# A cross-attention and mixture-of-experts layer on one core: normalised tiles split before they are turned, and turned by DMA

## The reference

```
x = x + xattn(layernorm(x), ctx)          # 16 heads of 32, causal, softmax over 64 keys
x = x + ffn(layernorm(x))
ffn(x):  logits = x @ router_w.T          # 8 experts, top 2 taken, weighted by their logits
         y_e = (silu(x @ wg_e) * (x @ wu_e)) @ wd_e
         out = sum of the chosen y_e * logit  +  shared expert (with biases)
```

## Time and profile before

| | us |
|---|---|
| runs shown | 870.81, 870.39, 866.59; median 870.39 |
| the profiled execution | 872.62 |
| its span in the trace | 870.9 |
| mean granted clock of TensorE | 0.979 of full |
| busy: TensorE, VectorE, ScalarE, GpSimd | 791.0, 614.5, 439.7, 429.2 |

### The profile page before, as it was taken

One profiled execution on the slowest core, in us unless ns is written; L12 is line 12 of the kernel. 1 busy time (PEld: TensorE's weight loads), 2 busy tenths in 40 slices (PEclk: granted clock), 3 DMA queues, 4 the chain that ended last, 5 costly groups with the idle time before them and its releaser, 6 DMA issues.

```text
span 870.9 us, 22280 instructions
## 1 busy us (share of the span) xinstructions
PE 791.0 (91%) x7516; PEld 545.4 (63%) x7516; DVE 614.5 (71%) x1196; ACT 439.7 (50%) x805; POOL 429.2 (49%) x530
## 2 busy tenths in 40 slices
PE   4478988989898989898999999999999999999994
PEld 1367776777777768687787787545555455455552
DVE  4978886989898989886557877555555555555552
ACT  3375766777777777777533553333333333333331
POOL 1144856565656656654600001255555555656553
PEclk9789998999999999999999999999999999999998
DMA  9324272635353534334575666488989889988892
GB/s 316 107 73 144 98 218 96 203 118 201 101 211 112 193 118 127 111 108 134 189 249 183 196 197 204 105 142 147 157 145 154 147 142 160 145 146 148 144 149 42
DMA packets 102760, 132.39 MB, mean 152 GB/s; under 512 B 54368, under 2 KB 55392, under 8 KB 101280
## 3 DMA queue, kind: packets, MB, share of 16 engines
q1 hardware_dynamic: 86784, 95.74, 37.3%
q0 software_dynamic: 15904, 35.70, 24.2%
HBM read 71.61 MB, written 52.31 MB: 142 GB/s over the span
## 4 chain that ended last, share of the span: by engine, by line
PE 46%; DVE 6%; ACT 4%; DMA 4%; issue 3%; POOL 3%; POOLq 0%; another core or an unknown queue 0%; ACTq 0%; DVEq 0%; SPq 0%
PE psum L1264 34%; PE psum L1312 8%; PE psum L1255 4%; DMA hidT<-xn2T_f 3%; DVE head_max L995 1%; DVE xy L1005 1%; DVE stats L926 1%; ACT probsT L700 1%; POOL rstd L532 1%; POOL kv_store L568 1%; ACT xn2T L700 1%; DVE w_q L1244 0%; PE psum L1364 0%; DVE hid L1219 0%; ACT attnT L700 0%
## 5 line engine op out<-in xcount | busy, mean ns | idle before, releaser
L680 POOL DMA_INDIRECT out<-w_q,tabs x71 | 112.5, 1584 | 109.1 <-DVE w_q L1244 72.9
L670 POOL DMA_INDIRECT x_in<-normed_tokens,tabs x71 | 71.0, 1000 | 137.6 <-DVE tabs L1130 88.2
L1229 DVE SCALAR_TENSOR_TENSOR hid<-psum,tabs,silu_g 128x256 f32<-128x256 f32 x71 | 34.4, 484 | 110.3 <-ACT silu_g L824 110.3
L1264 PE MATMUL psum<-exp_all,hidT 128*128 x426 | 103.4, 379 | 4.7 <-DMA hidT<-xn2T_f 4.7
L824 ACT ACTIVATE silu_g<-psum,tabs 128x256 f32<-128x256 f32 x71 | 33.7, 474 | 145.0 <-PE psum L1264 134.8
L1312 PE MATMUL psum<-xn1T,w_q 128*128 128x128 f16 x1536 | 93.3, 222 | 6.7 <-DVE xn1T L862 6.7
L1264 PE MATMUL psum<-exp_all,probsT 128*128 x420 | 96.4, 379 | 0.0
L1312 PEld LDWEIGHTS psum<-xn1T,w_q 128*128 128x128 f16 x1536 | 88.5, 99 | 7.1 <-DVE xn1T L862 6.9
L1264 PE MATMUL psum<-w_o,attnT 128*128 128x512 f16 x384 | 88.7, 381 | 0.0
L1264 PEld LDWEIGHTS psum<-exp_all,hidT 128*128 128x128 f16 x426 | 41.7, 98 | 55.8 <-issue 7.7
L530 POOL TENSOR_SCALAR rstd<-moments 128x1 f32<-128x1 f32 x64 | 14.3, 223 | 120.2 <-DVE moments L931 112.8
(11 more groups left out here) (199 smaller groups left out, 1730.2 us busy)
## 6 DMA issues: line engine op xcount, KB each, us to landing
x_in<-x SPq DMA_DIRECT2D x64, 256.0 KB, 3.1
exp_all<-experts SPq DMA_DIRECT2D x8, 1536.0 KB, 8.5
out<-xy SPq DMA_DIRECT2D x32, 256.0 KB, 2.1
normed_tokens<-xn SPq DMA_DIRECT2D x32, 256.0 KB, 2.4
normed_turned<-xn2T SPq DMA_DIRECT2D x32, 256.0 KB, 2.0
w_q<-out SPq DMA_DIRECT2D x32, 256.0 KB, 2.9
out<-w_q SPq DMA_DIRECT2D x32, 256.0 KB, 2.6
probsT<-normed_turned SPq DMA_DIRECT2D x16, 256.0 KB, 3.4
```

Source lines behind the costliest of these rows:

```text
L670: pool.indirect_dma_start(x_in[:, t % 4, :], None, xn_dram, bass.IndirectOffsetOnAxis(gather_at[:, t:t + 1], 0)).then_inc(gathered[t % 4], 16)
L680: pool.indirect_dma_start(out, bass.IndirectOffsetOnAxis(add_at[:, t:t + 1], 0), y[:, t % Y_RING, :], None, bounds_check=TOKENS - 1, oob_i ...
L1229: dve.scalar_tensor_tensor(hid[:, :], psum[:, GU_BANK[m % 2], I:2 * I], up_scale_at[:, tm:tm + 1], silu_g[:, :], ALU.mult, ALU.mult).then_ ...
L1264: last = pe.matmul(dst, lhsT(a, c), rhs(z, c), start=(c == 0 and a == z == 0), stop=(c == n - 1 and a == 1))
```

## The change

Both normalised tiles are split on ScalarE (high) and GpSimd (low) while still unturned, into `xn1p` and `xn2p`, and SP turns both halves of a tile with one transposing DMA of 128x1024 float16. TensorE's eight transposes per step, three ScalarE copies from PSUM and VectorE's low half of `xn1T` are gone. The scale by 2^11 moves into the inverse deviation. The expert's weights arrive in three DMAs, in steps j = 0, 1, 2. On ScalarE, qT and the logits now come ahead of xn2; on VectorE the magnitudes come behind qT; SP stores `xn2T` one step later. Two of the four `hidT` buffers lie in `xn1p`, and `hid_parts` in `xn2p`.

```diff
+EXPERT_PARTS = ((0, GU // 2), (GU // 2, GU // 2), (GU, WE - GU))
...
-        hidT = sb("hidT", [P, 4, 2, CI, P], F16)
-        xn2T_f = sb("xn2T_f", [P, H])
-        hid_parts = xn2T_f[:, :].bitcast(F16).rearrange("p (r v i) -> p r v i", r=2, v=2)
+        xn1p = sb("xn1p", [P, 2, H], F16)
+        hidT_store = sb("hidT_store", [P, 2, 2, CI, P], F16)
+        hidT = [hidT_store[:, n, :, :, :] for n in range(2)] + [
+            xn1p[:, n, :].rearrange("p (v c q) -> p v c q", v=2, c=CI) for n in range(2)]
+        xn2p = sb("xn2p", [P, 2, H], F16)
+        hid_parts = xn2p[:, :, :].rearrange("p r (v i) -> p r v i", v=2)
...
@@ SP, step @@
                 if live(t3):
                     load_again(t3, j + 1)
+                if live(t6):
+                    sp.wait_ge(xn2_turned, 16 * (t6 + 1))
+                    sp.dma_start(xT_dram[bass.ds(t6 * P, P), :], xn2T[:, :, :, :].rearrange("p v c q -> p (v c q)")
+                                 ).then_inc(xT_stored, 16)
+                if live(t1):
+                    sp.wait_ge(xn1_parts, t1 + 1)
+                    wait(sp, q_mm, t1)
+                    sp.dma_start_transpose(xn1T[:, :, :, :].rearrange("p v c q -> p (v c) q"),
+                                           xn1p[:, :, :].rearrange("p v h -> p (v h)")).then_inc(xn1_turned, 16)
...
-                if j == 0 and e is not None:
-                    sp.wait_ge(expert_in, 16 * e)
-                    load_expert(e)
+                if j < 3 and e is not None:
+                    sp.wait_ge(expert_in, 16 * (3 * e + j))
+                    load_expert(e, j)
...
-                    sp.wait_ge(xn2T_ready, t5 + 1)
-                    sp.dma_start(xT_dram[bass.ds(t5 * P, P), :], xn2T[:, :, :, :].rearrange("p v c q -> p (v c q)")
-                                 ).then_inc(xT_stored, 16)
+                    sp.wait_ge(xn2_parts, t5 + 1)
+                    wait(sp, router_mm, t5)
+                    wait(sp, xT_stored, 16 * t5)
+                    sp.dma_start_transpose(xn2T[:, :, :, :].rearrange("p v c q -> p (v c) q"),
+                                           xn2p[:, :, :].rearrange("p v h -> p (v h)")).then_inc(xn2_turned, 16)
...
@@ GpSimd, inv_std @@
-                pool.tensor_scalar(rstd[:, which, 0:1], moments[:, which, 1:2], EPS, None, ALU.add).then_inc(ln_eps[which], 1)
+                pool.tensor_scalar(rstd[:, which, 0:1], moments[:, which, 1:2], EPS, X_UP ** -2, ALU.add, ALU.mult
+                                   ).then_inc(ln_eps[which], 1)
...
@@ GpSimd, step: at its start, and in place of the old subtraction @@
+                if live(t1):
+                    pool.wait_ge(xn1_hi, t1 + 1)
+                    pool.tensor_tensor(xn1p[:, 1, :], xn1[:, :], xn1p[:, 0, :], ALU.subtract).then_inc(xn1_parts, 1)
                 if live(tile):
                     inv_std(0, tile)
...
-                    pool.wait_ge(xn2T_hi, 2 * (t5 + 1))
+                    pool.wait_ge(xn2_hi, t5 + 1)
...
-                    pool.tensor_tensor(flat(xn2T[:, 1, :, :]), xn2T_f[:, :], flat(xn2T[:, 0, :, :]),
-                                       ALU.subtract).then_inc(xn2T_ready, 1)
+                    pool.tensor_tensor(xn2p[:, 1, :], xn2[:, (j + 1) % 2, 0:H], xn2p[:, 0, :],
+                                       ALU.subtract).then_inc(xn2_parts, 1)
...
@@ ScalarE, step: xn2 moved behind qT and the logits; then attnT, and @@
+                if live(t5):
+                    act.wait_ge(xn2_ready, t5 + 1)
+                    wait(act, xn2_turned, 16 * t5)
+                    copy(xn2p[:, 0, :], xn2[:, (j + 1) % 2, 0:H], 1.0, xn2_hi)
...
@@ (probsT as before) @@
-                if live(t5):
-                    act.wait_ge(xn2T_mm, t5 + 1)
-                    wait(act, xT_stored, 16 * t5)
-                    copy(flat(xn2T[:, 0, :, :]), bank(6), X_UP, xn2T_hi)
-                if live(t1):
-                    act.wait_ge(xn1T_mm, t1 + 1)
-                    copy(flat(xn1T[:, 0, :, :]), bank(7), X_UP, xn1T_hi)
-                if live(t5):
-                    wait(act, xn2T_ready, t5)
-                    copy(xn2T_f[:, :], bank(6), X_UP, xn2T_hi)
...
                 if live(tile):
                     act.wait_ge(ln_rstd[0], tile + 1)
+                    wait(act, xn1_parts, tile)
                     act.activation(xn1[:, :], x_in[:, j % 2, 0:H], ACT.Identity, bias=rstd[:, 0, 2:3],
                                    scale=rstd[:, 0, 1:2]).then_inc(xn1_ready, 1)
+                    act.wait_ge(xn1_ready, tile + 1)
+                    wait(act, xn1_turned, 16 * tile)
+                    copy(xn1p[:, 0, :], xn1[:, :], 1.0, xn1_hi)
...
@@ VectorE, step: magnitudes moved behind qT, and @@
-                if live(t1):
-                    dve.wait_ge(xn1T_hi, t1 + 1)
-                    low(flat(xn1T[:, 1, :, :]), bank(7), X_UP, flat(xn1T[:, 0, :, :]), xn1T_ready)
...
@@ VectorE, entry @@
-                    low(flat(xgT[n % 4][:, 1, :, :]), bank(XG_BANK[t % 2]), X_UP, flat(xgT[n % 4][:, 0, :, :]), xgT_ready)
+                    dve.tensor_tensor(flat(xgT[n % 4][:, 1, :, :]), bank(XG_BANK[t % 2]), flat(xgT[n % 4][:, 0, :, :]),
+                                      ALU.subtract).then_inc(xgT_ready, 1)
...
@@ TensorE, step @@
-                    pe.wait_ge(xn1T_ready, t2 + 1)
+                    pe.wait_ge(xn1_turned, 16 * (t2 + 1))
...
-                    pe.wait_ge(xn2T_ready, t6 + 1)
+                    pe.wait_ge(xn2_turned, 16 * (t6 + 1))
+                    wait(pe, logits_ready, t6)
...
-                if live(t5):
-                    pe.wait_ge(xn2_ready, t5 + 1)
-                    wait(pe, logits_ready, t5)
-                    transposes(bank(6), xn2[:, (j + 1) % 2, :], C, xn2T_mm)
-                if live(t1):
-                    pe.wait_ge(xn1_ready, t1 + 1)
-                    wait(pe, xn1T_ready, t1)
-                    transposes(bank(7), xn1[:, :], C, xn1T_mm)
```

More of the change, by code:

```diff
@@ L367, in load_again, with load_expert @@
                 sp.dma_start(x_in[:, 2 + j % 2, 0:H], x[bass.ds(tile * P, P), :]).then_inc(xr_loaded[j % 2], 16)
[L369 to L371 removed]
+            def load_expert(e, n):
+                start, size = EXPERT_PARTS[n]
+                sp.dma_start(exp_raw[:, bass.ds(e * WE + start, size)],
+                             experts[:, bass.ds(e, 1), start:start + size].rearrange("p o w -> p (o w)")
+                             ).then_inc(expert_in, 16)
             def through_dram(e):
@@ L457, in _ @@
             sp.dma_start(sd_bias[:, :], sd_b.partition_broadcast(P)).then_inc(bias_in, 16)
-            load_expert(0)
+            for n in range(3):
+                load_expert(0, n)
             for b in range(3):
@@ L582, in step @@
                 tile = TPB * b + j
-                t2, t3, t4, t5 = [tile - n for n in range(2, 6)]
+                t1, t2, t3, t4, t5 = [tile - n for n in range(1, 6)]
                 e, pieces = pieces_at(b, j)
+                if live(t1):
+                    pool.wait_ge(xn1_hi, t1 + 1)
+                    plain(pool)
+                    pool.tensor_tensor(xn1p[:, 1, :], xn1[:, :], xn1p[:, 0, :], ALU.subtract).then_inc(xn1_parts, 1)
                 if live(tile):
@@ L752, in step @@
                     copy(logits[:, bass.ds(t6, 1), :], psum[:, 6, 0:E], sc[:, S_R:S_R + 1], logits_ready)
+                if live(t5):
+                    act.wait_ge(ln_rstd[1], t5 + 1)
+                    wait(act, xn2_stored[(j + 1) % 2], 16 * (TPB // 2 * b + (j - 5) // 2))
+                    act.activation(xn2[:, (j + 1) % 2, 0:H], x1, ACT.Identity, bias=rstd[:, 1, 2:3],
+                                   scale=rstd[:, 1, 1:2]).then_inc(xn2_ready, 1)
                 if live(t4):
@@ L933, in expert_magnitudes @@
             def expert_magnitudes(e, n):
+                dve.wait_ge(expert_in, 16 * 3 if isinstance(e, int) and e == 0 else 16 * (3 * e + n + 1))
                 if n == 0:
-                    dve.wait_ge(expert_in, 16 * (e + 1))
                     wait(dve, e_mags_stored, 16 * e)
-                start, size = ((0, GU // 2), (GU // 2, GU // 2), (GU, WE - GU))[n]
+                start, size = EXPERT_PARTS[n]
                 plain(dve)
@@ L969, in step @@
                     stage_stats(0, x_in[:, j % 2, 0:H], tile)
-                if e is not None and j in ((1, 2, 3) if isinstance(b, int) and b == 0 else (0, 2, 3)):
-                    expert_magnitudes(e, max(0, j - 1))
                 if live(tile):
@@ L976, in step @@
                     low(flat(qT[:, 1, :, :]), bank(5), Q_DOWN, flat(qT[:, 0, :, :]), qT_ready)
+                if e is not None and j in ((1, 2, 3) if isinstance(b, int) and b == 0 else (0, 2, 3)):
+                    expert_magnitudes(e, max(0, j - 1))
                 if live(t4):
```

35 lines of the change are left out of this document (17 added, 18 removed).

## The result

The changed kernel takes **900.97 us** (median of four runs, 899.72 to 904.32) against 870.6 for the kernel before on the same chip: ratio 1.036, 95% interval 1.032 to 1.040. The forecast had the sign and the ring; its 883 us were 12 us of loss where 30 came.

What follows compares the result with a forecast made beforehand. A ring from x1 to x1 over ScalarE and VectorE bounded the dense half; a new ring through SP's turns adds 14 us over eight batches, early steps lose 2, the tail returns 4: 883 us on the median, eight-in-ten range 845 to 904.

Steps and rivals of the forecast that it cites:

- The x1 ring: Dense half, x1 to next x1 over ScalarE and VectorE: closes in 10.45 us without slack, about 9.5 after the change.
- Rival D: Dense half: TensorE was the bound after all, 836 us at best; its chance is inside Rival A's 0.30.
- L: Time of a new-size transposing DMA from issue to landing: 3.3 us, range 2.1 to 6.7.
- Rival A: Transposing DMAs are cheap, L about 2.1 us, or the wait is reached later: 855 us, down to 841; chance 0.30.
- a sign of being wrong: On SP: the forecast would be wrong if a transposing DMA's issue took 1.2 us at the new size.
- The new ring: Steps with weight pieces, through GpSimd's low half, SP's turn and ScalarE's copy and piece: 8.05 + L = 11.35 us.
- the batch's sum: Dense half, four x1 gaps of a batch: 46.55 us against 44.8, so +1.75 a batch and +14 over eight.
- gap after the scales: x1 gap after the expert's scales: set by VectorE, 11.48 less 0.6, so 10.9 us.
- the keys' gap: x1 gap holding GpSimd's four copies of keys: 12.35 us, against 12.31 before.
- the third: Third x1 gap of a batch, with weight pieces and the turn's wait: 12.0 us.
- the early steps: Three early steps in which GpSimd also splits the shared weights: a loss of 2 us.
- The tail: Six tail steps, TensorE full beside the first shared entries: 4 us gained from the removed transposes.

Runs made afterwards that it cites:

- run 1: The kernel before with only the change's reordering on ScalarE and VectorE (the reordered kernel): 861.57 us, ratio 0.990.
- run 8: The changed kernel with eight unread identity transposes on TensorE ahead of the router's product: 896.44 us, ratio 1.032.
- run 10: The changed kernel with GpSimd making xn1's low half for only 8 of 512 columns: 876.80 us, ratio 1.010.
- run 3: The changed kernel with xn2 turned on TensorE again, xn1 still by DMA: 889.21 us, ratio 1.022.
- run 14: The changed kernel with SP storing turned xn2 after issuing xn1's turn, and the router's product behind the scores: 894.43 us, ratio 1.031.
- run 15: The changed kernel with two split-xn1 buffers, its low half on VectorE, SP's store after xn1's turn, and a late router product: 875.25 us, ratio 1.009.
- run 12: The changed kernel with xn1 by DMA, two buffers and its low half on VectorE, xn2 back on TensorE: 877.76 us, ratio 1.011.

## Why the prediction was right in kind and short in size

**The bound before.** The x1 ring over ScalarE and VectorE, with TensorE's transposes off it, was right: no run without the transposes came below the reordered kernel that has them all, and taking two copies out of xn2's way (run 1) gave 1.3 us in an undisturbed batch at once (44.8 to 43.5). Eight transposes put back (run 8) did not lengthen the kernel. Rival D is out.

**L.** Forecast 3.3 us; measured 3.1 from issue to landing (median of 32 for xn1; the longest 5.3), and 4.4 for xn2, which stands behind plain transfers:

```profile
xn1T<-xn1p SPq DMA_TRANSPOSE x32, 3.1
xn2T<-xn2p SPq DMA_TRANSPOSE x32, 4.4
```

Plain stores of the same bytes landed in 2.1 us before and in 2.4 after, and none of the 64 turns in under 3.0. Rival A, which needed about 2.1, fell. The Trainium skill's sentence in "Advanced Engine Details and Errata", section "X-Bar Transpose (TRN2)", that transposing DMAs are as fast as regular ones, does not hold against these stores; against plain loads of x of the same bytes, which took 3.8 us in the median of the same trace, it does. L is right for a partly wrong reason: the forecast had the issue at about 2.2 us; it was 1.25, which the prediction itself had named as a sign of being wrong.

**The new ring.** 11.35 forecast; in each of the six batches two of the four intervals from one low half of xn1 to the next are 11.37 to 11.42. With the low half cut to 8 columns (run 10) the first of the two is 10.4 to 10.5, and some 22 us come back where 24 were expected. The other two intervals are the batch's joints: 16.1 to 17.6 us over the copies of keys, where the prediction's own marks give 15.05 (5.8 to 20.85), and 8.8 to 10.8 where they give 8.8.

**The term that was mis-sized** is the batch's sum. The means of five batches after, against the forecast: gap after the scales 13.1 against 10.9, the keys' gap 11.9 against 12.35, the third 12.9 against 12.0, the fourth 11.2 against 11.3. The failing step is "The step after the expert's scales is VectorE's: 11.48 less 0.6 is 10.9". The third gap is the second part of it: 12.0 to 12.6 at full clock, near the forecast, and 13.3 to 13.4 in the three batches where the granted clock was 0.87. One gap after the scales, with the low half and the turn ahead of it; its two x1's are the rows of L1027:

```profile
217.13 1.16 POOL L611 TENSOR_TENSOR xn1p<-xn,xn1p 128x512 f16<-128x512 f32 x1
...
218.53 1.49 SPq L403 DMA_TRANSPOSE xn1T<-xn1p  x1
...
221.46 0.74 DVE L1027 SCALAR_TENSOR_TENSOR xy<-psum,sc,x_in 128x512 f32<-128x512 f32 x1
...
222.64 1.45 SPq L431 DMA_TRANSPOSE xn2T<-xn2p  x1
...
223.13 2.85 PE L1335 MATMUL psum<-xn1T,w_q 128*128 128x128 f16 x48 [1.64 <-DMA xn1T<-xn1p]
...
227.98 0.46 PE L1287 MATMUL psum<-w_r,xn2T 128*128 128x8 f16 x12 [2.00 <-DMA xn2T<-xn2p]
...
228.76 1.65 PE L1278 MATMUL psum<-ident,probs 128*128 128x128 f32 x8
230.20 2.57 PE L1380 MATMUL psum<-kv_store,qT 128*128 128x256 f16 x12
...
235.41 0.75 DVE L1027 SCALAR_TENSOR_TENSOR xy<-psum,sc,x_in 128x512 f32<-128x512 f32 x1
```

By the estimate, VectorE's list would have let x1 come at 10.9. But the last low half of the step before came one ring period behind the one ahead of it, and its turn took 4.6 us from the issue to the start of q, so q starts 1.67 us after x1 and not 0.33, as in the earlier trace rows. In the five batches this turn took 4.5 to 5.3 us and not the 3.1 of the median, at a share of the DMA engines of 0.83 to 1.05 over the gap that follows (0.49 to 0.79 before). The router then waits 2.00 us for a turn issued at 222.64 and landed 5.3 us later; and the stretch behind it has a granted clock of 0.62:

```profile
228.00:232.50 4.50, 4.50 (x35) 3.82 (x36) 2.83 (x6) 3.82 (x8) 2.16 (x4) 0.62 1.00 249
```

that is largely at the lower of the two levels, after TensorE had been idle for 1.64 and 2.00 us; the scores took 2.57 us there and 1.47 at 216.39, at full clock. I had summed this gap on VectorE alone and taken TensorE's side as given, while the sum of the other gaps went through every engine. Run 10 shows the low half in this gap as well (0.9 us). Runs 3, 8 and 14 each take one part of it away (gaps of 12.0, 12.3 and 12.6), none the whole; with all repairs (run 15) it is 11.7. How the 2.2 us divide between the late turn, the router's wait and the clock, no run tells.

**The rest of the difference.** The spans differ by 31.7 us: 1.2 up to the first x1, 7.4 to the sixth, 22.0 in the 24 steps (forecast 10.5), 0.8 less in the last two, 1.9 behind. For the 7.4 the forecast had 2 for the early steps and 2.2 for a batch and a quarter; they are steps in which GpSimd also splits the shared weights. That this is the same ring with longer parts is argued and not shown; run 15 has 60.5 us there and run 12 59.3, against 58.6 before and 66.1 after. The tail gave nothing back where 4 were forecast: the four x1's of its first four steps took 43.95 us before and 47.05 after (two of these steps are among the 24). In the prediction's list on GpSimd the parts add up to 37.4, not 37.6; nothing hangs on it.

**What cost nothing, as forecast:** the three-part loads, the reordered lists (a gain) and the new forms in the expert half, 446.7 against 448.6 us behind the last x1, and 441.0 to 446.6 in the other thirteen traces with them. Whether the new forms gain a few microseconds there was not tested by itself.

## What to carry to other kernels

Taking work off a nearly full engine helps only if that engine is in the ring that sets the period; follow the next period's first instruction back before paying for it elsewhere. A DMA in place of an engine's transpose adds its latency **and** a place in SP's, GpSimd's and a copy engine's order: sum the new ring, and sum **every** gap on every engine it passes, the ones that look bound by another engine too. A change of several parts should be timed by part: here its reordering alone was a 1% gain, and the rest hid it.

## What the runs showed that I had not expected

- A transposing DMA of 128x1024 float16 held SP for 1.25 us (median of xn1's 32; 1.39 for xn2's), one of half the size 1.19: the issue hardly grew with the size. Landing was 3.1 us, and 4.5 to 5.3 in the stretches in which the DMA engines were busiest.
- Eight idle-filling transposes per step did not make the kernel longer, and the granted clock of the dense windows went from 0.95 to 0.98. Single gaps show the price of the lower clock, before the change too: 12.3 us at full clock, 13.98 at 0.88, 15.93 at 0.79.
- A VectorE subtraction with both operands in SBUF took 0.68 us alone and up to 1.70 beside GpSimd, and GpSimd's instruction beside it 0.51 instead of 0.19. The Trainium skill, "GPSIMD Engine Reference", in its table of the engine, says that GpSimd's SBUF interfaces are shared with VectorE and that VectorE's instructions with two SBUF inputs contend for them; the trace agrees.
